# Autocorrelation stage: DFTs around the middle of a batch from sums and differences of its halves, products of 1024 columns, and a new order of the unit

## The reference

```python
qf = jnp.fft.fft(q, axis=2)
kf = jnp.fft.fft(k, axis=2)
corr = jnp.fft.ifft(qf * jnp.conj(kf), axis=2).real
topk = int(C * np.log(L))
w, idx = jax.lax.top_k(corr.transpose(0, 1, 3, 2), topk)
w = jax.nn.softmax(w, axis=-1)
...
for i in range(topk):
    g = jnp.minimum(idx[:, :, None, :, i] + pos, L - 1)
    out = out + w[:, :, None, :, i] * jnp.take_along_axis(v, g, axis=2)
...
x = x + jnp.tanh(g_xattn[1]) * _L1_xattn_ref(_layernorm(x, axis=-1), ctx_4096, ctx_4096)
```

## Time and profile before

| | |
|---|---|
| median of 3 runs | 2270.62 us (2267.35 to 2271.98) |
| the profiled execution, its own time | 2267.95 us |
| its span | 2266.2 us |
| PE busy over the span | 2153.9 us (95%) |
| DVE, ACT, POOL busy over the span | 1112.2, 1157.1, 424.3 us |
| autocorrelation: from its first vector instruction to its last | 1599.84 to 2042.69 us |

### The profile page before, as it was taken

How to read it: one execution, slowest core, us unless ns; L and a number is a source line. 1 busy time by engine, 2 the same in 40 slices (tenths; PEclk the granted TensorE clock), 3 DMA queues, 4 the chain that set the end, 5 groups by cost and what they waited for, 6 DMA issues and landing times. The chain is left out here.

```text
span 2266.2 us, 26427 instructions
## 1 busy us (share of the span) xinstructions
PE 2153.9 (95%) x10082; PEld 1076.0 (47%) x10082; DVE 1112.2 (49%) x2047; ACT 1157.1 (51%) x1823; POOL 424.3 (19%) x444
## 2 busy tenths in 40 slices
PE   7882999999999999999999999999799999988999
PEld 6761444444444444444444444444355555544444
DVE  6883242442525252432525252434577777756443
ACT  5667656656565665656565665653233343324111
POOL 1111211112121211112121211211132223321000
PEclk9995999999999999999999999999999999999999
DMA  5433111121111111111111111111200000000111
GB/s 191 165 116 110 52 56 53 47 62 47 52 56 47 56 53 52 51 57 47 56 52 54 55 47 53 56 47 66 93 19 19 19 19 19 19 0 1 50 50 50
DMA packets 55374, 125.52 MB, mean 55 GB/s; under 512 B 8336, under 2 KB 8720, under 8 KB 55120
## 3 DMA queue, kind: packets, MB, share of 16 engines
q1 hardware_dynamic: 55248, 123.84, 16.6%
HBM read 115.42 MB, written 8.39 MB: 55 GB/s over the span
## 5 line engine op out<-in xcount | busy, mean ns | idle before, releaser
L614 ACT ACTIVATE level<-level 128x512 f32<-128x512 f32 x924 | 581.8, 630 | 29.3
L791 PE MATMUL ps_ring<-xT_hi,gu_hi 128*128 128x512 f16 x1376 | 522.5, 380 | 2.0 <-DVE rel L718 2.0
L791 PE MATMUL ps_ring<-xT_lo,gu_hi 128*128 128x512 f16 x1376 | 522.2, 380 | 0.0
L791 PE MATMUL ps_ring<-xT_hi,gu_lo 128*128 128x512 f16 x1376 | 522.1, 379 | 0.0
L707 DVE SCALAR_TENSOR_TENSOR wt<-level,w_scale,absm 128x512 f32<-128x512 f32 x132 | 98.8, 748 | 496.0 <-ACT level L614 496.0
L726 DVE SCALAR_TENSOR_TENSOR X<-ps_ring,ffn_gain,X 128x512 f32<-128x512 f32 x352 | 260.1, 748 | 145.1 <-PE ps_ring L812 145.1
L812 PE MATMUL ps_ring<-dn_hi,hid_hi 128*128 128x512 f16 x704 | 266.9, 379 | 0.0
L812 PE MATMUL ps_ring<-dn_hi,hid_lo 128*128 128x512 f16 x704 | 266.8, 379 | 0.0
L812 PE MATMUL ps_ring<-dn_lo,hid_hi 128*128 128x512 f16 x704 | 266.7, 379 | 0.0
L668 POOL TENSOR_TENSOR gu_lo<-wt,gu_hi 128x512 f16<-128x512 f32 x88 | 102.7, 1167 | 766.7 <-ACT gu_hi L620 766.7
L791 PEld LDWEIGHTS ps_ring<-xT_hi,gu_lo 128*128 128x128 f16 x1376 | 134.6, 98 | 163.2 <-issue 1.1
(11 more groups left out here) (200 smaller groups left out, 2828.5 us busy)
## 6 DMA issues: line engine op xcount, KB each, us to landing
codes<-in_codes SPq DMA_DIRECT2D x132, 256.0 KB, 2.8
absm<-in_absmax SPq DMA_DIRECT2D x264, 128.0 KB, 3.0
X<-in_x SPq DMA_DIRECT2D x16, 512.0 KB, 4.1
c_in<-in_ctx SPq DMA_DIRECT2D x16, 512.0 KB, 5.1
cT<-in_ctxT SPq DMA_DIRECT2D x16, 512.0 KB, 3.5
xT_hi<-in_ctx SPq DMA_DIRECT2D x8, 1024.0 KB, 4.8
out<-X SPq DMA_DIRECT2D x16, 512.0 KB, 2.6
w<-in_w SPq DMA_DIRECT2D x1, 4096.0 KB, 14.4
```

The costliest lines, as they stand in the source:

```text
L614: act.activation(level[u % 2][:], codes[u % RING][:] if k == 0 else level[u % 2][:], ACT.Prelu, bias=bias, scale=scale, alpha=alpha).then_ ...
L791: mm = pe.matmul(o[:], w[c][:, m, k, :], xx[:, k, ts], start=(q == 0), stop=(q == 3 * KD - 1))
```

## The change

The host hands in the rows 128 to 255 of each batch of x and of the context in reverse (`turned`), and turns the result back. A cosine or sine about the middle of the batch is then the same for row t of the first tile and row t of the second, up to a sign, so a DFT of 256 rows becomes one product over 128 rows of the sum of the two tiles, or of their difference:

- `k_fold` (POOL) makes `diff` (128 x 512) and overwrites the first context tile with the sum; `k_fix` (DVE) adds and subtracts twice the last row of the batch, which a DMA (`load_last`) spreads over all partitions. `k_even` and `k_odd` (PE) need 2 float32 products each, where `spectra_in` had 4 and 4.
- `q_fold` and `q_low` (POOL) make the sum and difference of the normalised tiles and the low float16 part, one unit at a time; `q_spectrum` has 6 products for 12. `q_low` leaves the DVE.
- `w_fold` (POOL) makes sum and difference of the two halves of the delays, the second one read backwards, in 8 instructions of 128 x 128; `weight_turn` transposes them, and `weight_dfts` has 12 products for 24.
- The multiplications of real and imaginary parts work on both at once: `products` is 2 instructions of 128 x 1024 for 4 of 128 x 512, `weight_products` 4 for 8. The copies of the spectra are one of 1024 columns for two of 512.
- The order of the unit: the PE does `weight_turn(n)`, `weight_dfts(n)`, `corr(n+1)`, `output(n)`, `k_even(n+2)`, `q_spectrum(n+2)`, `k_odd(n+2)`; the DVE does `products(n+2)` last in unit n, and `k_fix(n+3)` ahead of it.

How many instructions there are of `corr`, `select`, `output`, `out_comb` and `add` is unchanged.

The core of the diff, on SP and POOL:

```diff
+                def load_last(n):
+                    if n >= 2:
+                        sp.wait_ge(kfix_done, 2 * n - 2)
+                    sp.dma_start(last[n % 2], io["ctx"][n // 2, P, cols(n)].partition_broadcast(P)).then_inc(last_in[n % 2], 16)
...
+                for n in range(2):
+                    load_last(n)
...
                 for name in ("lora1_a", "lora1_b", "mag", "w1"):
                     sp.dma_start(res[name][:], io[name]).then_inc(res["w1_in"], 16)
-                for m in range(1, B // 2):
-                    for s in range(2):
-                        sp.wait_ge(out_mm, 4 * m - 2 + 2 * s + FIRST)
-                        sp.dma_start(c_in[s], c_d[2 * m + s]).then_inc(ctx_in[s], 16)
+                for n in range(2, N):
+                    load_last(n)
+                    if n % 2 == 0 and n >= 4:
+                        sp.wait_ge(u_mm, n - 2)
+                        sp.dma_start(c_in[(n // 2) % 2], c_d[n // 2]).then_inc(ctx_in[(n // 2) % 2], 16)
...
+                def k_fold(n):
+                    x0, x1 = (raw(n)[:, t, cols(n)] for t in range(2))
+                    pool.wait_ge(ctx_in[(n // 2) % 2], 16 * (n // 4) + 16)
+                    if n >= 2:
+                        pool.wait_ge(u_mm, n - 1)
+                    pool.tensor_tensor(diff[n % 2][:], x0, x1, ALU.subtract).then_inc(kf_done, 1)
+                    pool.wait_ge(kf_done, 2 * n + 1)
+                    pool.tensor_tensor(x0, x0, x1, ALU.add).then_inc(kf_done, 1)
+                def q_fold(n):
+                    pool.wait_ge(xn_done, 2 * (n // 2) + 2)
+                    pool.wait_ge(qlo_done, n)
+                    pool.tensor_tensor(qf[:, 0, :], xn[:, 0, cols(n)], xn[:, 1, cols(n)], ALU.add).then_inc(qf_done, 1)
+                    pool.tensor_tensor(qf[:, 1, :], xn[:, 0, cols(n)], xn[:, 1, cols(n)], ALU.subtract).then_inc(qf_done, 1)
+                def q_low(n):
+                    pool.wait_ge(qhi_done, n + 1)
+                    pool.tensor_tensor(q_lo[n % 2][:], qf[:], q_hi[n % 2][:], ALU.subtract).then_inc(qlo_done, 1)
...
+                    pool.wait_ge(prod_done, 2 * n + 1)
+                    pool.tensor_tensor(t_d[:, 0, :], t_d[:, 0, :], t_d[:, 1, :], ALU.add).then_inc(prod_comb, 1)
+                    pool.wait_ge(prod_done, 2 * n + 2)
+                    pool.tensor_tensor(t_x[:, 1, :], t_x[:, 1, :], t_x[:, 0, :], ALU.subtract).then_inc(prod_comb, 1)
...
+                def w_fold(n):
+                    if n:
+                        pool.wait_ge(wT_mm, n)
+                    for c in range(CH):
+                        pool.wait_ge(w_done, CH * n + c + 1)
+                        for k, op in enumerate((ALU.add, ALU.subtract)):
+                            pool.tensor_tensor(wf[:, k, c, :], cut2[:, c, 0:P], cut2[:, c, P:L][:, ::-1], op).then_inc(wf_done, 1)
...
                 rstd_of(0)
+                k_fold(0)
+                q_part(0)
+                k_fold(1)
                 corr_comb(0)
+                q_part(1)
                 rstd_of(1)
...
+                k_fold(2)
+                w_fold(0)
+                q_part(2)
+                for n in range(N):
+                    if n + 1 < N:
+                        corr_comb(n + 1)
+                    out_comb(n)
+                    if n + 3 < N:
+                        q_fold(n + 3)
+                        k_fold(n + 3)
+                    if n + 1 < N:
+                        w_fold(n + 1)
+                    if n + 3 < N:
+                        q_low(n + 3)
+                    if n % 2 == 0 and n // 2 + 2 < B:
+                        rstd_of(n // 2 + 2)
```

On ScalarE, TensorE and VectorE (the lines taken out of their order, and out of `select` and `output`, are left away where they are in the listing above):

```diff
+                spectrum_out(1)
                 corr_row(0)
+                q_high(1)
+                exps(0)
+                q_norm(1)
+                q_high(2)
                 weights(0)
...
+                for n in range(N):
+                    weights_T(n)
+                    if n + 1 < N:
+                        corr_row(n + 1)
+                    out_row(n)
+                    if n % 2 == 1 and n + 3 < N:
+                        q_norm((n + 3) // 2)
+                    if n + 3 < N:
+                        q_high(n + 3)
+                    if n + 1 < N:
+                        exps(n + 1)
+                        weights(n + 1)
+                    if n + 2 < N:
+                        spectrum_out(n + 2)
...
+                def k_even(n):
+                    pe.wait_ge(kfix_done, 2 * n + 2)
+                    if n >= 2:
+                        pe.wait_ge(wprod_done, 4 * n - 6)
+                        pe.wait_ge(k_done, n)
+                    dft(1, 0, raw(n)[:, 1, cols(n)])
+                    dft(1, 1, diff[n % 2][:]).then_inc(k_mm, 1)
+                def k_odd(n):
+                    if n >= 2:
+                        pe.wait_ge(wprod_done, 4 * n - 4)
+                        pe.wait_ge(u_done, n)
+                    dft(2, 0, diff[n % 2][:])
+                    dft(2, 1, raw(n)[:, 0, cols(n)]).then_inc(u_mm, 1)
+                def q_spectrum(n):
+                    pe.wait_ge(qlo_done, n + 1)
+                    if n >= 2:
+                        pe.wait_ge(x_done, 2 * n - 2)
+                    if n == 1:
+                        pe.wait_ge(prod_done, 2)
+                    for half in range(2):
+                        mm = dft_parts(0, half, 0, q_hi[n % 2][:, half, :], q_lo[n % 2][:, half, :])
                     mm.then_inc(q_mm, 1)
...
+                    for c in range(CH):
+                        pe.wait_ge(wn_done, CH * n + c + 1)
+                        for h in range(2):
+                            mm = pe.transpose(ps[3][:, h, c * P:(c + 1) * P], wf[:, h, c, :], ident[:])
                     mm.then_inc(wT_mm, 1)
...
+                    pe.wait_ge(k_done, min(n + 2, N))
+                    for half in range(2):
+                        mm = dft_parts(1, half, 0, wT_hi[:, half, :], wT_lo[:, half, :])
                     mm.then_inc(ws_mm, 1)
-                    pe.wait_ge(u_done, 2 * n + (4 if nxt else 2))
-                    for half in (re, im):
-                        mm = dft_parts(2, half, 1, lambda t: wT_hi[:, t, :], lambda t: wT_lo[:, t, :])
+                    pe.wait_ge(u_done, min(n + 2, N))
+                    for half in range(2):
+                        mm = dft_parts(2, half, 1, wT_hi[:, 1 - half, :], wT_lo[:, 1 - half, :])
                     mm.then_inc(ws_mm, 1)
...
+                    for k, src in enumerate((e_d, e_x, n_d, n_x)):
+                        pe.wait_ge(wprod_comb, 4 * n + k + 1)
                         for t in range(2):
...
+                            mm = pe.matmul(ps[0][:, t, :], inv[:, k, t * P:(t + 1) * P], src[:, 0, :], start=(k == 0), stop=(k == 3))
                     mm.then_inc(out_mm, 1)
...
+                k_even(0)
+                q_spectrum(0)
+                k_odd(0)
+                pe.wait_ge(k_done, 1)
+                k_even(1)
+                pe.wait_ge(u_done, 1)
+                k_odd(1)
                 corr(0)
...
+                q_spectrum(1)
+                for n in range(N):
+                    weight_turn(n)
+                    weight_dfts(n)
+                    if n + 1 < N:
+                        corr(n + 1)
+                    output(n)
+                    if n + 2 < N:
+                        k_even(n + 2)
+                        q_spectrum(n + 2)
+                        k_odd(n + 2)
...
+                def k_fix(n):
+                    both = raw(n)[:, 0, cols(n)]
+                    dve.wait_ge(last_in[n % 2], 16 * (n // 2) + 16)
+                    dve.wait_ge(kf_done, 2 * n + 2)
+                    dve.scalar_tensor_tensor(raw(n)[:, 1, cols(n)], last[n % 2], 2.0, both, ALU.mult, ALU.add).then_inc(kfix_done, 1)
+                    dve.wait_ge(kfix_done, 2 * n + 1)
+                    dve.scalar_tensor_tensor(both, last[n % 2], -2.0, both, ALU.mult, ALU.add).then_inc(kfix_done, 1)
...
+                def products(n):
+                    k = k_sp[n % 2]
                     dve.wait_ge(q_mm, n + 1)
-                    dve.wait_ge(k_done, 2 * n + 2)
-                    if not (isinstance(n, int) and n == 0):
+                    dve.wait_ge(k_done, n + 1)
+                    if n:
                         dve.wait_ge(corr_mm, n)
-                    for dst, a, b_ in ((t_rr, re, k_re), (t_ii, im, k_im), (t_ir, im, k_re), (t_ri, re, k_im)):
-                        dve.tensor_tensor(dst[:], ps[0][:, a], b_[par][:], ALU.mult).then_inc(prod_done, 1)
+                    dve.tensor_tensor(t_d[:], ps[0][:], k[:], ALU.mult).then_inc(prod_done, 1)
+                    dve.tensor_tensor(t_x[:], ps[0][:], k[:, ::-1, :], ALU.mult).then_inc(prod_done, 1)
...
+                def weight_products(n):
+                    if n:
+                        dve.wait_ge(out_mm, n)
+                    for k, (pair, sp, d, x) in enumerate(((1, k_sp, e_d, e_x), (2, o_sp, n_d, n_x))):
```

(21 more changed lines are left out.)

301 lines of the change are left out of this document (94 added, 207 removed).

## The result

The changed kernel took 2275.31 us (median of 8 runs, 2270.87 to 2277.01), the kernel before beside it 2268.18 (8 runs, 2267.35 to 2271.98): a ratio of 1.0026, 95% interval 1.0016 to 1.0036, slower by about a quarter of a per cent. The profiled execution took 2274.37 us, its span is 2272.6; that of before took 2267.95 with a span of 2266.2. So 6.4 us have to be found.

A forecast was written before the change was run, and what follows sets the result against it. PE bounds the kernel before; after the change a ring through the DVE does. Head +15.0, steps -6.6, tail -2.6 give +5.8 us on the profiled 2267.95, 2273.8, plus 2.7 to the median: 2276 us, range 2250 to 2304.

The forecast's parts named there:

- The bound moves from PE to a ring through the DVE: In the steps, PE's work falls from 25.9 to 18.6 us; weight_products, select, add, q_spectrum form one ring that sets the pace.
- A unit without stalls, and the meetings: One step takes 24.8 us with stats, 22.2 without, plus 0.7 for two DVE instructions meeting POOL's at SBUF.
- `w_fold` runs 12.9 to 16.3 on POOL and ACT scales by 16.8: Within a unit, times in us from the start of weight_dfts: the weights' fold and scaling are done in time.
- The clock: PE's idle gaps make its clock fall to 1.2 of 2.4 GHz, each fall costing about 2.1 us.
- a fall in each of the 6 steps: Steps with stats: PE idles 5.1 us ahead of weight_dfts, so the clock falls each time, 2.1 us a step.
- I count half, 1.1 us, in the others: Steps without stats: PE idles 2.5 us and shortly before 1.0, counted as half a clock fall, 1.1 us a step.
- rival 2: Clock falls come only in the steps with stats: 9.9 us off the forecast, 2266 us; chance 20%.
- Sum of the steps: The 15 steps: 6 x 27.6 + 8 x 24.0 + 21.4 = 379.0 against 385.55 us, 6.6 us gained.
- Head: Stage start up to the first weight_dfts: 53.9 us for 38.88, 15 us lost; first transposes at 50 for 34.7.
- Tail: Stage end from the last weight_dfts: output ends at 14.3, add at 15.8 us for 18.43, 2.6 us gained.
- From the profile to the median: The median of the runs lies 2.7 us above the profiled execution, so 2273.8 us becomes 2276.
- Rival 3: POOL becomes the bound: small w_fold sums at 0.7 us give 2306 us, or complete SBUF exclusion 2300; chance 23%.

The follow-up runs named there:

- e11: e8 with the statistics in one piece behind add in every second unit, and 20 instead of 3 extra matmuls behind k_odd in the units that follow: 2243.64 us.
- e10: e8 with each of the six products of 1024 columns of a unit cut in two of 512: 2228.46 us.
- e8: e7 with extra matmuls, results unread, in what is left of PE's gaps in every unit (8 ahead of q_spectrum, 3 behind k_odd): 2224.50 us.
- e5: The changed kernel with POOL's w_fold waiting for all four weight instructions of select instead of one after the other: 2294.23 us.
- e4: The changed kernel with k_odd moved behind the weight transposes and, on ACT, k_out (copy of k_even's result) ahead of the weights: 2258.56 us.
- e12: e8 with the row maximum nmax on ACT, 5 instead of 8 extra matmuls ahead of q_spectrum, and more extra matmuls at the stage's two ends: 2217.34 us.
- e3: The changed kernel with only the head in another order (batch 1 statistics and normalization, w_fold(0), products(1) and weights(0) earlier): 2267.24 us.
- e1: The changed kernel with the next batch's statistics taken one tile a unit behind weights_low, where the DVE waits: 2267.70 us.
- e7: The changed kernel with e1, e3 and e4 together (statistics spread, head reordered, k_odd behind the transposes): 2239.36 us.

## Why the prediction was right, and where two errors met

2276.0 was forecast and 2275.31 measured; but terms of the sum are off by up to 8 us, and cancel. That the total fits to 0.7 us is luck.

- *The bound moves from PE to a ring through the DVE*: right. It was seen in the gaps that end with the DVE, and tested: of the statistics 18 us of 20 expected show in the steps (e11), of the cutting of products 3.0 of 6.5 (e10), while PE got 154 more matmuls in e8 without a loss.
- *A unit without stalls, and the meetings*: forecast 25.5 with `stats` (24.8 + 0.7) and 22.9 without; measured 26.0 to 26.4 and, less the 1.55 of a fall, 23.4. The step that failed is "`w_fold` runs 12.9 to 16.3 on POOL and ACT scales by 16.8". Its price alone was right, 3.34 us in e5 for 3.4; beside the weight instructions eight folds took 3.76 to 4.67, and `select` 8.8 to 9.2 us for 7.9, so the fold ended at 17.9 (1829.45 less 1811.60). I had priced the meetings on the DVE's side only, at 0.7 a step where they cost it 1.0 to 1.5 (`nmax`, the weight instructions, `k_fix`), and on POOL's side not at all. Behind the fold, on ACT, stands `k_out`, for which the DVE waited 1.86 us; `products` was not done at 20.2. e5 shows how hard this chain pulls; e4, which took `k_out` out of it and moved `k_odd`, gave 16.8 us.
- *The clock*: "a fall in each of the 6 steps" was right by count. Its price was 1.55 us in the four steps of 24.93, and so 2.2 and 2.3 in the two of 25.56 and 25.70 us, for 2.1 forecast; "I count half, 1.1 us, in the others" was wrong: none fell before the last step. 22.5 us were counted and some 15 came: 10.7 in the six falls, 2.3 in the first step, whose 12 rows took 5.09 us for 2.76 at the low clock that it inherits from the head, and some 1.7 in the last. That is rival 2's clock; rival 2's time didn't come because the ring was longer.
- *Sum of the steps*: 379.0 against 378.67, by these two errors of opposite sign, the clock counted some 7.5 us too high and the ring as much too low: the six with `stats` 158.8 instead of 165.6, the other eight 197.6 instead of 192.0, the last 22.3 instead of 21.4. (e12 shows that the low clock in the first step is the head's: filling the head took 2.05 us off that step.)
- *Head*: +17.05 for +15.0. The order was read rightly (the transposes at 51.6 us for 50) and e3 took half of the loss back by order alone.
- *Tail*: 0.69 gained for 2.6. `output` was to end at 14.3; it began at 7.4 as forecast, but its first eight rows ran at the low clock (2.81 and 2.77 us for four, 1.88 at the full clock), and it ended at 16.2. Where they didn't, in e3, the tail took 16.0 us, near the forecast.
- *Left out*: the next stage, 2.7 us shorter by its clock alone. Nothing in the sum stood for it, and it is no gain of the change: in the profiles of e1, e3, e4, e10 and e11, where this stage is the same program, it took 223.4 to 223.8 us again.
- *From the profile to the median*: 2.7 us were added, by three runs of the kernel before. Over its 8 runs the median lies 0.2 above the profiled execution (2268.18 and 2267.95), and the changed kernel's 0.9 above its own. By the profiles the change cost 6.4 us for 5.8 forecast, by the medians of 8 runs 7.1; the term that was too large hid this.
- *Rival 3, complete exclusion*: the mechanism is there, its price is not, because few instructions meet a long sum. The Trainium skill ("SBUF — State Buffer", "Who interferes with whom") says that a DVE instruction with two SBUF inputs and a GpSimd one that reads SBUF exclude each other for a whole instruction, and that a `tensor_scalar` within SBUF can do so too. The row of `nmax` above (1.01 us) and the one of e8 below agree, and so did the pair in the earlier trace rows, which I misread: the cost of a meeting is what is left of the other's instruction, less some 0.13 to 0.2 us. There 0.56 was left and 0.36 paid, at `nmax` 0.98 (1821.88 less 1820.90) and 0.85. I took 0.36 as the price of any meeting. (The range's upper end, 2304, also lies a little under the 2306 that this rival works out to.)

So a change that took 86 us of busy time from PE moved the steps by 7, for two reasons that the runs show: the pace went over to a ring through the DVE, POOL and ACT, which the change loads more, and the clock takes part of the gain back as long as PE has gaps (some 5 of 12.6 us in e1; 15 us between e7 and e8).

## What to carry to other kernels

When work is taken from TensorE and another engine sets the pace, count what the gaps cost: in this kernel a fall of the clock was worth 1.3 to 2.3 us, filling one gap moved the fall to the next, and filling all of them, with matmuls whose results nobody reads, removed it; how much less would do wasn't tried. An order that was right for an engine that was full has to be laid anew for the one that is full now: three moves of order, none of which takes work away, gave 36 us where the change itself had lost 7. And when a sum comes out right, check its terms: here two errors of some 7.5 us each cancelled.
